# Cross attention of a Perceiver block: where TensorE puts the result products of a batch's first and second unit

## What is computed

```python
q = split_heads(queries @ Wq + bq)
k = split_heads(keys @ Wk + bk)
v = split_heads(values @ Wv + bv)
scores = jnp.einsum('bhqd,bhkd->bhqk', q, k) / jnp.sqrt(jnp.float32(HD))
scores = jnp.where(mask, jnp.float32(-1000000000000000.0), scores)
attn = jax.nn.softmax(scores, axis=-1)
ctx = jnp.einsum('bhqk,bhkd->bhqd', attn, v)
...
return ctx @ Wo + bo
```

## Time and profile before

| | |
|---|---|
| median of 3 runs | 2890.74 us (2889.43 to 2891.78) |
| the profiled execution | 2892.8 us |
| its span, first to last instruction | 2891.1 us |
| TensorE (PE) matmuls busy | 2660.4 us, 92% of the span |
| TensorE weight loads (PEld) busy | 2075.1 us, 72% |
| VectorE (DVE) busy | 1671.3 us, 58% |
| ScalarE (ACT) busy | 1441.8 us, 50% |
| mean granted TensorE clock | 0.965 |
| cross attention stage, about | 850 to 2320 us of the span |

### The profile page before, as it was taken

One profiled execution on the slowest core, in us unless ns is written; L12 is line 12 of the kernel. 1 busy time (PEld: TensorE's weight loads), 2 busy tenths in 40 slices (PEclk: granted clock), 3 DMA queues, 4 the chain that ended last, 5 costly groups with the idle time before them and its releaser, 6 DMA issues. The chain is left out here.

```text
span 2891.1 us, 58626 instructions
## 1 busy us (share of the span) xinstructions
PE 2660.4 (92%) x24696; PEld 2075.1 (72%) x24696; DVE 1671.3 (58%) x3485; ACT 1441.8 (50%) x2943; POOL 114.1 (4%) x104
## 2 busy tenths in 40 slices
PE   6999899899869999999999999999999987789987
PEld 3444677789757887778777877778777765667764
DVE  4333542557565555665655556655556678864487
ACT  2112222336435566565665656656666622725775
POOL 0000200120010000000000000000000013010000
PEclk9999999999979999999999999999999988899988
DMA  7998102347751011111111111111111020114300
GB/s 257 311 311 282 48 4 66 125 147 268 235 171 30 20 48 49 47 26 26 49 48 47 26 26 49 48 41 31 26 49 39 31 63 1 40 44 161 117 16 30
DMA packets 202932, 249.40 MB, mean 86 GB/s; under 512 B 77728, under 2 KB 132000, under 8 KB 202416
## 3 DMA queue, kind: packets, MB, share of 16 engines
q1 hardware_dynamic: 193456, 220.49, 24.2%
q10 hardware_dynamic: 6656, 16.78, 1.8%
q0 software_dynamic: 2560, 8.39, 0.8%
HBM read 221.50 MB, written 24.12 MB: 85 GB/s over the span
## 5 line engine op out<-in xcount | busy, mean ns | idle before, releaser
L91 PE MATMUL xa_J<-xa_c_hi,xa_wk_hi 128*128 128x402 f32 x1024 | 369.9, 361 | 1.7 <-POOL xa_m L2491 1.7
L2380 DVE TENSOR_TENSOR cl_v<-xa_J,main_x 128x512 f32<-128x512 f32 (+1 forms) x208 | 143.5, 690 | 390.2 <-PE xa_J L93 301.5
L93 PE MATMUL xa_J<-xa_c_hi,xa_wk_lo 128*128 128x402 f32 x1024 | 354.7, 346 | 0.0
L92 PE MATMUL xa_J<-xa_c_lo,xa_wk_hi 128*128 128x402 f32 x1024 | 354.5, 346 | 0.0
L2245 ACT ACTIVATE xa_kT<-xa_J,cl_bk 128x402 f32<-128x402 f32 x256 | 151.5, 592 | 383.7 <-PE xa_J L93 380.5
L91 PE MATMUL xa_J<-xa_wv_hi,xa_c_hi 128*128 128x512 f32 (+1 forms) x832 | 339.0, 407 | 0.4 <-ACT xa_kT L2245 0.4
L93 PE MATMUL xa_J<-xa_wv_hi,xa_c_lo 128*128 128x512 f32 (+1 forms) x832 | 327.7, 394 | 0.0
L92 PE MATMUL xa_J<-xa_wv_lo,xa_c_hi 128*128 128x512 f32 (+1 forms) x832 | 327.2, 393 | 0.0
L2258 ACT ACTIVATE xa_pr<-xa_pr,xa_nm 128x416 f32<-128x416 f32 x512 | 321.5, 631 | 3.9 <-DVE xa_nm L2364 3.9
L2264 ACT ACTIVATE xa_pr<-xa_pr,xa_ri 128x416 f32<-128x416 f32 x512 | 280.1, 630 | 60.4 <-DVE xa_ri L2368 60.1
L2354 DVE CUSTOM_DVE_ANT_0 xa_pr<-xa_S,xa_m 128x416 f32<-128x416 f32 x512 | 271.8, 587 | 43.6 <-PE xa_S L2536 29.3
(11 more groups left out here) (516 smaller groups left out, 4962.2 us busy)
## 6 DMA issues: line engine op xcount, KB each, us to landing
bl_rows<-in_ctx SPq DMA_DIRECT2D x40, 1024.0 KB, 8.8
main_x<-in_ctx_cols SPq DMA_DIRECT2D x192, 201.0 KB, 2.6
bl_cols<-in_ctx_cols SPq DMA_DIRECT2D x24, 1024.0 KB, 10.5
moe_raw<-in_L_ffn_routed_w SPq DMA_DIRECT2D x45, 512.0 KB, 4.8
main_qoT<-in_L_ffn_w ACTq DMA_DIRECT2D x32, 512.0 KB, 4.0
main_x<-in_ctx_cols SPq DMA_DIRECT2D x64, 197.5 KB, 3.3
main_qoT<-in_L_attn_W SPq DMA_DIRECT2D x16, 512.0 KB, 3.7
routed_in<-main_qoT SPq DMA_DIRECT2D x1, 7680.0 KB, 22.6
```

What stands on the lines that cost most here:

```text
L91: pe.matmul(out, w_hi, x_hi, start=first, stop=False)
L92: pe.matmul(out, w_hi, x_lo, start=False, stop=False)
L93: return pe.matmul(out, w_lo, x_hi, start=False, stop=last)
L2380: nc.vector.tensor_tensor(v[0:rows(n), value_slot(b, n), :], J[0:rows(n), place(b, ("v", n)) % 2, :], bv_sb[0:rows(n), :], ALU.add)\
```

## The change

Two lists change: TensorE's, and ScalarE's, which has to follow TensorE's order. `result(w)`, for the first unit of a batch, leaves the end of its batch and comes after the first key tile of the next batch (where it is called `result(w - 4)`). `result(w - 3)`, for the second unit, was there and moves behind the second key tile, before `spread_max(w - 1)`. On ScalarE `keep_key` now comes before `keep_result` at both places. The last batch's own results stay where they were, at the end of the stage, so the 15 seams between batches change and nothing else.

```diff
@@ ScalarE
                     if b:
                         highs(b, 3, 0, 2)
+                        keep_key(w, 0)
                         keep_result(w - 4)
-                        keep_key(w, 0)
                         highs(b, 3, 2, 4)
+                        keep_key(w, 1)
                         keep_result(w - 3)
-                        keep_key(w, 1)
                         probabilities(w)
@@ TensorE
                     if b:
                         key_tile(w, 0)
-                        result(w - 3)
+                        result(w - 4)
                         send_max(w - 1)
                         key_tile(w, 1)
+                        result(w - 3)
                         spread_max(w - 1)
                         key_tile(w, 2)
                         key_tile(w, 3)
@@ TensorE, end of a batch
                     if not last:
                         value_tile(b, 12)
-                        result(w)
```

## The result

The changed kernel takes 2864.2 us (median of 4 runs, 2862.35 to 2867.38); the kernel before took 2890.09 us (median of 4). The ratio is 0.9912, 95% interval 0.9895 to 0.9929: faster by 25.9 us, where 28.2 were forecast. A later comparison of the same two kernels, beside experiment 8, gave 2862.68 and 2891.11 us, 28.4 us apart. The profiled execution took 2863.34 us, with a span of 2861.6 against 2891.1. One execution of all those reported here, of the kernel of experiment 1, took 4239.5 us at a mean granted clock of 0.58, where its other four had 0.965 to 0.967, and no ratio counts it.

A forecast was written before the change was run, and what follows sets the result against it. TensorE's own list was taken to set the stage's pace, waiting 1.58 us per seam. Seams of 8.24 instead of 10.12 us, 15 x 1.88 = 28.2 us, bring 2890.74 to 2862.5 us; range 2859.5 to 2868.5.

The forecast's parts named there:

- its one wait at a seam: TensorE's first result waits for VectorE's copy of value tile 12 out of PSUM: 1.58 us at each of 15 seams.
- The sum for a seam: From value tile 12's last matmul to the third key tile: 8.24 us instead of 10.12, so 1.88 us shorter.
- The pair not seen before: `spread_max` directly behind a result, until the third key tile starts: priced at 0.15 us, with ends of 0.03 and 0.42.
- The changeovers: On TensorE from a key tile into a result: 0.27 us each, as in the trace.
- the tile's own pace of 0.18 us into a result: If TensorE pulls weight loads ahead, a result behind a key tile starts sooner: seam 2 x 0.09 us shorter, forecast 2.7 lower.
- The sum of the seams: Fifteen seams between batches, each 1.88 us shorter, give 28.2 us.
- The thinnest margin: Value tile 12's copy is out before the first result needs it, with 0.54 us left; without cover the wait returns.
- The other margins: Key banks, `largest`, emptied `O`, context split and exponentials are in time; `largest` 3 us early, exponentials 2.4 us ahead of `sums`.
- The wait coming back in part: Rival: less rest on ScalarE and VectorE delays tile 12's copy by 1 us; 6.9 us lost, 2869.4 us; chance 0.06.
- No gain: Rival: the softmax chain holds the period, TensorE's wait only moves to `sums` or the scores; 2890.7 us; chance 0.03.
- The drop of the clock: Rival: the granted clock drops once pauses go or move, 5.1 us lost per seam; 2939 us; slower, chance 0.03.
- the second result finds it empty: ScalarE's copy out of `O` is done at about 1031.6, while the second result would start at 1033.60.

The follow-up runs named there:

- experiment 8: Changed kernel with the third unit's result also moved, in front of the next `spread_max`: 2861.24 us; repeated, 2859.38 us beside 2862.68 for the changed kernel.
- experiment 1: Changed kernel with the second move taken back, both results behind key tile 0: 2879.68 us against 2891.34 before, ratio 0.9962; run again, 2874.69 us.
- experiments 3 and 4: Changed kernel with VectorE's copy of value tile 12 later, behind two context splits, or also behind two transposes: 2872.52 and 2885.24 us against 2891.34 before.
- experiment 5: Changed kernel with ScalarE's four lines back in the old order, `keep_result` before `keep_key`: 2864.57 us against 2891.94 before, ratio 0.9907.
- experiment 7: Changed kernel with `spread_max` put ahead of the second result: 2864.29 us against 2891.94 before, ratio 0.9908.
- experiment 3: Changed kernel with VectorE's copy of value tile 12 behind two context splits: 2872.52 us against 2891.34 before, ratio 0.9934.
- the shift: Both results behind key tile 0, plus 128 waits on a long-set semaphore at the start of TensorE's stage list: 2892.21 us in one execution.

## Why the prediction was right

**What bounds the stage** was read rightly: TensorE's list sets the pace, and its one wait at a seam was worth its whole length. The period fell from 91.2 to 89.4 us.

**The sum for a seam** was 8.24 us and is 8.28, with one at 8.33. The 0.04 are in two pieces: key tile 1 took 2.11 us instead of 2.09, and a changeover 0.28 instead of 0.27; the rest is rounding. The pair not seen before, `spread_max` behind a result, was priced at 0.15 us and took 1029.78 - 1029.63 = 0.15, not the 0.03 or 0.42 of its ends. The changeovers stayed at 0.27 and 0.28, and the tile's own pace of 0.18 us into a result, which the page "TensorE: Matmul & The Clock Gate" of the Trainium skill, Part 2 (What happens when you issue a matmul), would have allowed by the prediction's reading, was not reached at any seam.

**The sum of the seams.** In the traces the 15 seams together take 152.2 us before and 124.2 after, 28.0 less, against 28.2 forecast. The whole spans differ by 29.5 us. The medians differ by 25.9 us in the first comparison and 28.4 in the second, so 2862.5 forecast stands beside 2864.2 and 2862.68 measured. What lies between these numbers is the scatter of executions, several us for one kernel (2862.35 to 2867.38): outside of the seams the two traces differ by 2.1 us ahead of the stage and by 2.1 us the other way behind it, in code that is the same.

**What had to be on time** was on time. The thinnest margin was about 0.6 us (0.54 forecast), and experiments 3 and 4 show that it is real and that past it the loss is one for one. The other margins were wide: the key copies may come later (experiment 5), and `spread_max` may stand on either side (experiment 7).

**The rivals.** The wait coming back in part is a true mechanism, shown by experiment 3 with 0.41 us at each seam, but the change stays clear of it. "No gain" fell with the period, and with `sums`, at which no wait appeared. The drop of the clock fell with 1.00 in the stretches of 89.40 us. The idea behind the first of them, that the copy of tile 12 comes later against TensorE when VectorE and ScalarE lose rest, fell too: VectorE lost 1.83 us of it, and the copy still starts 1.23 us behind the tile's last matmul.

**What the prediction didn't weigh** is why the second result had to move as well. It counted the two moves as one sum. Experiment 1 shows that the first alone is worth less than half, 11.7 us, since two results in a row wait for `O` and break off inside the second. For `O` the prediction had checked that the second result finds it empty in the new order, so it was right there by its working. Stops inside a result it did not look for, though the kernel before has one of 1.6 us at the end of the stage. That the seams of the changed kernel stay almost free of them was luck.

## What to carry to other kernels

If the busiest engine waits for a copy of what it has just made, put work between that needs neither, and lay the stretch out again from rows of the same pairs: here that forecast 28.2 us, and the seams gave 28.0. Check first how far ahead of its new user the copy ends, since past this margin the wait returns one for one. Keep bursts of very short matmuls apart, and place each next to other small ones, where the change from large tiles is paid already.

## What the runs showed that was not expected

Two results in a row, 208 matmul records and as many weight loads in some 3.6 us, stop in about half of the seams at no semaphore. The second then takes 0.3 to 2.5 us more than its 1.59. One result alone, which was all that stood between larger tiles, did this rarely and briefly: 8.33 us instead of 8.28 at one of the 15 seams of the changed kernel, 10.33 and 10.29 instead of 10.12 at two before the change, and at most 0.35 us in the other kernels. Which seams stop depends on the place in the instruction stream: 128 spare waits, executed once, moved the stops to other seams.

Two of the longest stops at a seam also cost clock. Behind idle times of 1.62 us (seam 7 of experiment 1) and 1.89 us (seam 4 with the shift) the granted clock was 0.50, the lower level of 1.2 GHz, from 1484.8 to 1488.0 and from 1220.1 to 1223.3 us, and the matmuls of the key tile there start 0.33 us apart instead of 0.18. The 15 pauses of 1.58 us in the kernel before did not do this: it has 1.00 from 935 to 2215 us.
